# Reordering the five engine programs within a turn of a gated delta-rule recurrence

## What is computed

```python
q, k, v = silu(causal_conv(h @ Wq)), silu(causal_conv(h @ Wk)), silu(causal_conv(h @ Wv))
k = k / norm(k)
alpha, beta = sigmoid(h @ Wa + ba), sigmoid(h @ Wb + bb)
def step(S, (kt, vt, qt, at, bt)):
    upd = vt - at * (S @ kt)
    S = clip(at * S + bt * outer(upd, kt), -5, 5)
    return S, S @ qt
x = x + ga * ((y * silu(h @ Wg + bg)) @ Wo)
x = x + gb * moe(layernorm(x) * (1 + cb) + sb)
```

## Time and profile before

| | us |
|---|---|
| median of three runs | 1870.27 |
| lowest, highest | 1864.04, 1873.93 |
| profiled execution, its span | 1869.6 |
| clear of X, first to last of the 14 full turns | 128.76 to 1109.60 |
| DVE, PE, POOL, ACT busy in these 980.84 us | 859.18, 897.28, 735.08, 565.95 |

### The profile page before, as it was taken

One profiled execution on the slowest core, in us unless ns is written; L12 is line 12 of the kernel. 1 busy time (PEld: TensorE's weight loads), 2 busy tenths in 40 slices (PEclk: granted clock), 3 DMA queues, 4 the chain that ended last, 5 costly groups with the idle time before them and its releaser, 6 DMA issues. The chain is left out here.

```text
span 1869.6 us, 59680 instructions
## 1 busy us (share of the span) xinstructions
PE 1620.9 (87%) x24736; PEld 1142.6 (61%) x24736; DVE 1389.8 (74%) x1892; ACT 895.2 (48%) x1768; POOL 1127.0 (60%) x1362
## 2 busy tenths in 40 slices
...
GB/s 184 49 53 25 69 91 37 67 93 37 67 92 37 67 93 36 67 93 36 69 92 36 65 75 26 69 144 227 135 128 110 46 230 79 94 93 100 96 91 51
DMA packets 89465, 156.59 MB, mean 84 GB/s; under 512 B 15708, under 2 KB 54116, under 8 KB 88108
## 3 DMA queue, kind: packets, MB, share of 16 engines
...
## 5 line engine op out<-in xcount | busy, mean ns | idle before, releaser
L1386 PE MATMUL d_ps<-hT,turn_shared 128*128 128x512 f32 x768 | 402.8, 632 | 8.4 <-DVE d_Vp L1171 4.6
L953 POOL TENSOR_TENSOR turn_shared<-turn_shared,d_tmp 128x31 f32<-128x31 f32 (+15 forms) x496 | 289.7, 584 | 38.9
L948 POOL TENSOR_TENSOR d_tmp<-turn_shared 128x31 f32<-128x31 f32 (+15 forms) x496 | 286.4, 577 | 38.9
L1024 DVE SCALAR_TENSOR_TENSOR turn_shared<-d_ps,d_cw,turn_shared 128x1023 f32<-128x1023 f32 (+2 forms) x192 | 245.3, 1278 | 15.0 <-ACT turn_shared L682 12.6
L742 ACT ACTIVATE d_S<-d_S,gamma_chunk 128x64 f32<-128x64 f32 x448 | 130.9, 340 | 184.5 <-DVE d_S L1052 144.6
...
L1386 PEld LDWEIGHTS d_ps<-hT,turn_shared 128*128 128x128 f32 x768 | 126.8, 192 | 87.6 <-issue 71.4
L2526 ACT ACTIVATE m_hm<-m_ps,m_b_tile 128x128 f32<-128x128 f32 x284 | 80.9, 368 | 206.3 <-PE m_ps L2706 206.3
L122 PE MATMUL o_po<-wo_split,y_high 128*128 128x256 f32 x512 | 101.7, 302 | 44.8 <-DVE y_low L115 44.8
L2549 POOL DMA_INDIRECT out<-m_yo,m_slot_i x71 | 114.2, 1608 | 41.2 <-issue 20.3
L2696 PE MATMUL m_ps<-m_w,m_xs 128*128 x284 | 136.2, 602 | 1.6 <-DVE m_xs L2641 1.0
L2287 POOL TENSOR_TENSOR y<-y,g_sb 128x512 f32<-128x512 f32 x48 | 78.8, 1676 | 94.7 <-ACT g_sb L2271 94.7
...
## 6 DMA issues: line engine op xcount, KB each, us to landing
...
y_scratch<-d_yT SPq DMA_DIRECT2D x256, 64.0 KB, 1.8
d_arow<-ab_scratch SPq DMA_DIRECT2D x128, 128.0 KB, 3.1
...
```

Source lines behind the costliest of these rows:

```text
L948: nc.gpsimd.tensor_tensor(tv, Tq[:, s + 1:, s].rearrange("p (r a) -> p r a", a=1).broadcast_to([P, left, known]), X[:, s, 0:known].rearran ...
L953: nc.gpsimd.tensor_tensor(X[:, s + 1:, 0:known], X[:, s + 1:, 0:known], tv, ALU.subtract).then_inc(s_sub, 1)
L1024: nc.vector.scalar_tensor_tensor(out=dst[:, j + 1:], in0=src[:, 0:T - 1 - j], scalar=cw[:, u // BP % 2, n, 2 - j:3 - j], in1=dst[:, j + 1: ...
L1386: return nc.tensor.matmul(dst[:, g, :], w[:, m % 2, n, dc, :], hT[:, dc, at:at + G], start=(dc == 0), stop=(dc == DC - 1))
```

## The change

All five programs keep their instructions, and 14 turns of the loop do the same work. The lists per c become one written-out order per turn, in another sequence on every engine. On DVE decay(un, 1) goes from behind largest_k to before state 12, and state 13 and turn_y(tc, 2) go behind the two transposes of X. On PE the step 14 of the chain goes behind cross_second, and step 15 in between the two halves of kk. On ACT silu_k(un, 0) goes ahead of first_k(un, 1), and carry_state(tc, 14) between keep_x and keep_cross. On POOL gamma_k changes places with bound_terms(tb, 1). On SP step_rows(un, 1) goes up, alpha_rows and the load of Wg (gate_weights) change places. In the last turns the gate's products stand later.

On SP:

```diff
                 if bound:
                     store_y(tb, 1)
-                if bound:
-                    alpha_rows(tb, 1)
-                if chain:
-                    store_y(tc, 0)
                 if new_k:
                     step_rows(un, 1)
-                if it + 2 < TURNS:
-                    step_rows(it + 2, 0)
-                if chain:
-                    alpha_rows(tc, 0)
+                if chain:
+                    store_y(tc, 0)
                 if prep and u % BP == BP - 1 and u // BP + 2 < M:
                     weights(u // BP + 2)
                 if it == TURNS - 1:
-                    sp.wait_ge(s_qproj, 4 * TURNS)
-                    sp.wait_ge(s_D, 2 * TURNS)
-                    sp.dma_start(wg_raw, wg).then_inc(s_gw, 16)
+                    gate_weights()
+                if bound:
+                    alpha_rows(tb, 1)
+                if chain:
+                    alpha_rows(tc, 0)
+                if it + 2 < TURNS:
+                    step_rows(it + 2, 0)
```

On ACT, the end of a turn:

```diff
-                    if new_k and c == 14:
-                        first_k(un, 1)
-                    if prep and c == 14:
-                        keep_cross_first(u)
-                        keep_x(u)
-                        keep_cross(u)
-                    if new_k and c == 14:
-                        silu_k(un, 0)
-                        silu_k(un, 1)
-                    if prep and c == 14:
-                        keep_w(u, 0)
+                if new_k:
+                    silu_k(un, 0)
...
+                if chain:
+                    keep_u(tc, 13)
+                if new_k:
+                    first_k(un, 1)
+                if prep:
+                    keep_cross_first(u)
...
+                if prep:
+                    keep_x(u)
+                if chain:
+                    carry_state(tc, 14)
+                if prep:
+                    keep_cross(u)
...
+                if new_k:
+                    silu_k(un, 1)
+                if chain:
+                    keep_u(tc, 14)
+                if prep:
+                    keep_w(u, 0)
```

On POOL:

```diff
                 if prep:
                     clear_x(u)
                     solve(u)
+                    gamma_k(u)
                 if bound:
                     bound_terms(tb, 1)
                 if prep:
-                    gamma_k(u)
                     decay_k(u, 0)
                     decay_k(u, 1)
```

On DVE, the lines added at the end of a turn (the old order there is in the rows below):

```diff
+                if new_k:
+                    tap_k(un, 0, 2)
+                    decay(un, 1)
+                if chain:
+                    state(tc, 12)
...
+                if prep:
+                    rows_of_x(u)
+                    turn_x(u)
+                if new_k:
+                    tap_k(un, 1, 0)
+                if chain:
+                    state(tc, 13)
```

On PE, the lines added at the end of a turn:

```diff
+                if prep:
+                    cross_first(u, 0)
+                    cross_first(u, 1)
+                if chain:
+                    state_sum(tc, 13)
+                if prep:
+                    cross_second(u, 0)
+                    cross_second(u, 1)
...
+                    state_into_u(tc, 14)
...
+                if prep:
+                    w_product(u, 0)
...
+                if chain:
+                    state_sum(tc, 14)
+                    y_of_u(tc, 6)
...
+                if chain:
+                    seed_u(tc, 15)
+                if new_k:
+                    kk(un, 0)
+                if chain:
+                    y_of_state(tc, 7, 0)
+                    state_into_u(tc, 15)
+                if new_k:
+                    kk(un, 1)
```

712 lines of the change are left out of this document (418 added, 294 removed).

## The result

The changed kernel takes 1946.87 us (median of 4 runs, 1943.40 to 1950.38) against 1869.16 for the kernel before (4 runs, 1864.04 to 1873.93): ratio 1.0427, 95% interval 1.0406 to 1.0447. It is 78 us slower. I had forecast 1876, with a range up to 1893. The profiled execution spans 1941.8 us against 1869.6.

What follows compares the result with a forecast made beforehand. POOL's substitution, or PE by a little, bounds the solve (clear of X to last subtraction), DVE's chain the tail; 14 x (1.4 - 0.4) = +14, minus 8, is +6 on 1869.6: 1876 us, range 1854 to 1893.

Steps and rivals of the forecast that it cites:

- The second scan in the solve: Moving decay(un, 1) ahead of state 12 stretches POOL's substitution by 1.9 us; L1183 starts at 47.0 against 45.6: +1.4 a turn.
- the vector engine stood ready and POOL was the last: Reading of the solve's end before the change: POOL's last subtraction ends at 458.00, L1183 starts at 458.03.
- POOL's exchange: gamma_k ahead of bound_terms in the tail: it ends 1.9 us earlier, but w_product waits for ACT's copies; no effect.
- SP's new order: step_rows(un, 1) ahead of the store of y, alpha rows later: nothing in the full turns.
- The tail: From L1183 to the next clear: DVE's chain 1.3 us shorter, mostly lost to PE; -0.4 us a turn, ends -2.1 and +0.9.
- From turn 15 on: Last turns: L1183 at 45.2 (up to -2), earlier Wg load (-3), earlier bound scans (-3); together -8 us.
- (c): Slower rival: PE bounds the tail, low clock 10 us and more; +2.1 a turn, 1892 or 1897 us; chance 0.21.
- if L1183 starts later than 47.6: Sign of being wrong, at the solve's end, in us behind the clear: DVE's or PE's chain would be the bound.

Runs made afterwards that it cites:

- k1: k0 with decay(un, 1) moved from the tail into the solve, to just ahead of state 13's old place: 1900.1 us, ratio 1.018 to the kernel before.
- k0: h1 with turn_y(tc, 2) and y_of_state(6, 0) moved behind the turn of X, scan in the tail: 1879.4 us, ratio 1.007 to the kernel before.
- h4: Old order on PE, ACT and DVE to step 8, changed from step 9; scan in the solve, SP's and POOL's orders changed: 1895.9 us, 1.018 to before.
- e2: The changed kernel with decay(un, 1) put back behind largest_k, in the tail: 1924.9 us, ratio 1.030 to the kernel before.
- e3: The kernel before with POOL's exchange alone, gamma_k ahead of bound_terms(tb, 1): 1867.9 us, ratio 0.999.
- e1: The changed kernel with POOL's exchange undone, bound_terms(tb, 1) ahead of gamma_k again: 1918.4 us, ratio 1.026 to the kernel before.
- h1: The kernel before to step 12, then the changed tail order on PE, ACT and DVE; SP's new order, scan in the tail: 1908.7 us, ratio 1.020.
- m_b_sp: The kernel before with SP's new order alone: 1925.8 us, ratio 1.030.
- h2: The same as h1 but with SP's old order: 1879.5 us, ratio 1.007 to the kernel before.

## Why the prediction was wrong, point by point

- **The second scan in the solve, +1.4 us a turn.** The mechanism and the size were right: k1 against k0 shows 1.84 us where I took 1.9, h4 has the turn of X at 46.8 where I put 47.0. What failed is the sentence "DVE's work in the solve becomes 40.8 us, which with the 5 us that it waits today would be 46: just below POOL". The work was right (40.6). The waits were taken over from an order that no longer holds; they are 6.9 us. They were also rounded down: the earlier trace rows have 45.00 - 39.47 = 5.5, so the margin under POOL's 46.8 was 0.5 us and not 0.8. It decided the case: DVE passed POOL's end by half a microsecond, and there the scan took 3.0 us more than its own length. Of the delay of a quiet turn the scan behind the solve makes 2.5 us and the late recurrence 3.1, by e2. The start of L1228 is 4.6 us later than before, not 1.4; over 14 turns the difference of 3.2 is 45 us.
- **"the vector engine stood ready and POOL was the last".** That reading of the turn from 413.13 was wrong, and it hid how thin the margin was. DVE came out of state 13, which had waited 1.00 us for PE, in the same 0.2 us in which POOL ended (timeline of DVE, before):

```profile
457.82 0.29 DVE L1052 TENSOR_TENSOR d_S<-d_S,d_ps 128x128 f32<-128x128 f32 x1 [1.00 <-PE d_ps L1633]
```

  State 13 waits 0.6 to 1.0 us for PE in each of the 14 turns before. In seven of them L1183 starts with POOL's end and state 13 0.1 to 0.2 us ahead of that; in the other seven L1183 starts 0.5 to 2.5 us behind POOL's end, right behind state 13. So the recurrence bounded half of the solves already, and POOL the other half by 0.2 us.
- **POOL's exchange, "Nothing".** Right in the old order (e3: 0.999). In the changed kernel it costs 28 us (e1), since it puts a product of 3.68 us instead of 1.93 where the late scan falls. I asked who waits for gamma_k, and not whom gamma_k holds up.
- **SP's new order, nothing in the full turns.** In the changed kernel no turn_y waits for a store, because turn_y(tc, 2) moved as well (k0 against h1 shows what that is worth; the changed kernel with SP's old order was not run). In the old order it costs 56 us (m_b_sp). I had not followed the store of y that the steps' rows were put ahead of.
- **The tail, -0.4 us a turn.** It came out at +0.8. In the undisturbed tails of h4 (three of 22.5 to 22.8 us, against 23.8) the gain is there, and larger than I took. The changed kernel's mean tail is 2.5 us longer than those three. 1.0 us of this are PE's issue gaps of 0.8 us and more, 13.9 us over its tails against 7.1 before. Some 0.6 us go with the low clock, which begins earlier and lasts 12.2 us a tail instead of 9.7, after PE stood for the locked-out scan (e1). The rest is open, and so is what makes the gaps; h2, with less of the low clock than before, has a longer tail all the same.
- **From turn 15 on, -8 us.** It was 0 (760.1 against 760.0). The Wg load was issued 17.9 us earlier in the turn and PE's wait of 2.92 us is gone. But the turn of X of that turn started at 47.2, not at 45.2, and the last bound scan still waits for its rows, 3.60 us. Timeline of DVE:

```profile
1312.17 1.39 DVE L1129 TENSOR_TENSOR_SCAN d_ps<-d_arow,d_carry,d_ps 128x256 f32<-128x256 f32 x2 [3.60 <-DMA d_arow<-ab_scratch]
```

- **The rivals.** None of them was it. (c), the slower side, had PE and a long low clock in the tail and ended at 1892. The sentence that I would be wrong "if L1183 starts later than 47.6, which would mean that DVE's or PE's chain, not POOL, is the bound" names the case, and it should have been a rival with a price. With the measured start, 50.5 - 45.6 = 4.9 us a turn, it is 1938.
- **The sum by the runs.** From the changed kernel, 51 us are the order of the first eight steps (h4), and with it the scans that it pushed behind the solve. What is left, 23 us by the spans (1892.7 against 1869.6), is 14 times 1.2 us in the solve and 0.5 in the tail.
